# One gather column in 56 moved from GpSimd's indirect DMAs to SyncE, row by row

## The reference

```python
z = h @ W_fc.T                       # 12500 x 64
z_src, z_dst = z[src], z[dst]        # 200000 x 64 each
a = z_src @ blk[0] + z_dst @ blk[K] + ex @ w_e + ...      # moments add a constant
att = jnp.where(a > 0, a, SLOPE * a)
m = jax.ops.segment_max(att, dst, num_segments=N)
expv = jnp.exp(att - m[dst])
w = expv / jax.ops.segment_sum(expv, dst, num_segments=N)[dst]
return jax.ops.segment_sum(w[:, None] * (z_src + ez), dst, num_segments=N)
```

## Time and profile before

| what | value |
|---|---|
| median of 3 runs | 4289.09 us (4285.36 to 4289.59) |
| the profiled execution | 4292.92 us |
| its span, first to last instruction | 4291.0 us |
| mean granted TensorE clock | 0.551 |
| busy in the span: PE, PE loads, DVE, ACT, POOL | 55%, 45%, 71%, 49%, 71% |
| POOL's gathers in the attention pass | 2267.4 to 4233.2 us |

### The profile page before, as it was taken

The page is one execution under the profiler, slowest core; times in us unless marked ns, Lnnn a source line. Parts: engine busy times, 40 slices in busy tenths (PEclk is TensorE's granted clock), DMA queues, the critical chain, the costliest instruction groups (busy, mean ns, idle before and its releaser), DMA issues.

```text
span 4291.0 us, 59828 instructions
## 1 busy us (share of the span) xinstructions
PE 2349.2 (55%) x12446; PEld 1922.5 (45%) x12447; DVE 3028.6 (71%) x9415; ACT 2107.1 (49%) x8940; POOL 3028.7 (71%) x3157
## 2 busy tenths in 40 slices
PE   4566666676878787889986333333333333333332
PEld 1344445554666676768866332222222222222222
DVE  8775556666677777878755777777767777777776
ACT  2778777777776877732042333333333333333332
POOL 5777777777777777777106777777777777777773
PEclk6665565555555565655587555555555555555555
DMA  8653333333444454544302222222222222222222
GB/s 231 166 142 100 91 83 79 91 88 83 95 97 95 96 110 95 114 98 104 67 15 41 37 37 36 36 36 35 36 36 36 36 36 36 35 36 36 36 35 81
DMA packets 726909, 308.31 MB, mean 72 GB/s; under 512 B 661869, under 2 KB 662029, under 8 KB 726480
## 3 DMA queue, kind: packets, MB, share of 16 engines
q1 hardware_dynamic: 612608, 160.26, 18.9%
q0 software_dynamic: 100032, 105.80, 12.0%
q10 hardware_dynamic: 13968, 39.17, 2.7%
HBM read 206.21 MB, written 98.73 MB: 71 GB/s over the span
## 4 chain that ended last, share of the span: by engine, by line
POOL 49%; issue 20%; PE 13%; DVE 9%; ACT 5%; DMA 3%; DVEq 1%; POOLq 0%; SPq 0%; ACTq 0%
POOL zg L637 30%; POOL sorted_dram L599 19%; PE half_banks L958 8%; DVE work L1304 2%; DMA z_sb<-sorted_dram 2%; ACT z_sb L694 1%; PE half_banks L1105 1%; DMA sorted_dram<-ea_sb,idx 1%; DVE oh_all L1228 1%; ACT ohp L710 1%; ACT ohj L712 1%; ACT half_banks L817 1%; PE half_banks L1040 1%; DVEq L1293 1%; DVE zg L1317 1%
## 5 line engine op out<-in xcount | busy, mean ns | idle before, releaser
L599 POOL DMA_INDIRECT sorted_dram<-ea_sb,idx x1563 | 1520.8, 973 | 504.1 <-issue 462.2
L637 POOL DMA_INDIRECT zg<-z_dram,idx x1563 | 1488.1, 952 | 520.7 <-issue 519.4
L958 PE MATMUL half_banks<-z_sb,zg 128*128 128x65 f32 x4736 | 1038.4, 397 | 407.8 <-DVE work L1304 398.1
L958 PEld LDWEIGHTS half_banks<-z_sb,zg 128*128 128x128 f32 x4736 | 987.2, 308 | 580.3 <-DVE zg L1317 568.5
L817 ACT ACTIVATE half_banks<-half_banks,f_s 128x80 f32<-128x80 f32 x1568 | 358.6, 316 | 764.6 <-DVE half_banks L1631 764.6
L1116 PE MATMUL low_banks<-ident,f_top 128*80 128x128 f32 x196 | 85.4, 436 | 1051.6 <-DVE f_top L1664 1051.6
L694 ACT ACTIVATE z_sb<-z_sb 128x98 f32<-128x98 f32 x1568 | 420.4, 270 | 407.0 <-DVE z_sb L1246 407.0
L1304 DVE TENSOR_TENSOR work<-work,half_banks 128x65 f32 x2368 | 510.6, 216 | 151.9 <-PE half_banks L958 67.7
L710 ACT ACTIVATE ohp<-trow,zg 128x128 bf16<-128x128 f32 x1568 | 476.9, 386 | 198.4 <-PE half_banks L936 198.4
L1116 PEld LDWEIGHTS low_banks<-ident,f_top 128*80 128x80 f32 x196 | 27.9, 142 | 1089.6 <-DVE f_top L1664 1089.6
L1317 DVE TENSOR_TENSOR zg<-half_banks,away 128x256 f32<-128x256 f32 x1184 | 492.9, 417 | 1.4 <-issue 0.7
(11 more groups left out here) (288 smaller groups left out, 3407.9 us busy)
## 6 DMA issues: line engine op xcount, KB each, us to landing
z_sb<-sorted_dram SPq DMA_DIRECT2D x592, 132.0 KB
ea_sb<-in_edge_attr_dram SPq DMA_DIRECT2D x195, 256.0 KB, 3.6
sorted_dram<-ea_sb,idx POOLq DMA_INDIRECT x1563
zg<-z_dram,idx POOLq DMA_INDIRECT x1563, 2.5
sorted_dram<-big_b ACTq DMA_DIRECT2D x4, 3333.0 KB, 19.8
sorted_dram<-big_b ACTq DMA_DIRECT2D x4, 3069.0 KB, 11.7
f_t<-t_dram SPq DMA_DIRECT2D x196, 40.0 KB, 2.9
sorted_dram<-big_b ACTq DMA_DIRECT2D x4, 1353.0 KB, 10.7
```

Source lines behind the costliest of these rows:

```text
L599: g_.indirect_dma_start(out=sorted_dram[BUF[c]][:, :], out_offset=bass.IndirectOffsetOnAxis(ap=idx[0:n, m % 4, g:g + 1], axis=0), in_=ea_s ...
L637: g_.indirect_dma_start(out=zg[0:n, s, g, 0:ZW + 1], out_offset=None, in_=z_dram[:, :], in_offset=bass.IndirectOffsetOnAxis(ap=idx[0:n, s, ...
L958: ins = t_.matmul(banks[4 + n % 2][:, u * AW:(u + 1) * AW], oh_step[:, n % 2, u, :], es_sb[:, n % 4, u, 0:AW], start=True, stop=True)
```

## The change

In blocks of seven macros from the third block on (macro 14 and later, 26 blocks of 28), the last column (g = 7) of slot 1 is no longer fetched by POOL. SP fetches its 128 rows one by one, each with a DMA of its own whose address is in a register, into a buffer `row_z` (two halves, used in turn) in `ea_sb`, which is unused by then. ACT copies the 128x66 floats from there into the slot of `zg`, and DVE's `masks` waits for that copy in slot 1. The row numbers come from the input `src` by a small DMA into `row_ids`, one for each block.

The rows of a block are spread over the seven macros before the one that uses them: ROWS_IN[s] rows between the load of the table and the wait for `f_tabn`, ROWS_OUT[s] rows between the store and the wait for its landing.

```diff
+ROWS_IN, ROWS_OUT = (12, 12, 12, 12, 8, 8, 8), (8, 8, 8, 8, 8, 8, 8)
+        row_z = ea_sb[:, 2, 0:2, :]
+        row_ids = ea_sb.rearrange("p s g c -> p (s g c)")[0:1, 3 * G * EW:3 * G * EW + 2 * P].bitcast(I32)
...
+            def load_ids(j):
...
+                    sp.dma_start(row_ids[:, k * P:(k + 1) * P], ids.rearrange("(a p g) -> a p g", a=1, g=G)[:, :, G - 1]
+                                 ).then_inc(r_ids, 16)
+
+            def fetch_rows(k, p0, n):
+
+                for p in range(p0, p0 + n, 4):
+                    rows = nc.values_load_multi_w_load_instructions(
+                        row_ids[0:1, k * P + p:k * P + p + 4], [mybir.EngineType.SP], min_val=0, max_val=NODES - 1)[1]
+                    for u in range(4):
+                        sp.dma_start(row_z[p + u:p + u + 1, k, :], z_dram[bass.ds(rows[u], 1), :]).then_inc(r_land[k], 16)
+
+            def update_rows(it, q, fetch=None):
                 m = it * U + q
                 row = row_of(m)
                 sp.dma_start(tab[0:W, :], tab_dram[bass.ds(row, W), :]).then_inc(f_rows, 16)
+                if fetch is not None:
+                    k, s = fetch
+                    fetch_rows(k, sum(ROWS_IN[:s]) + sum(ROWS_OUT[:s]), ROWS_IN[s])
                 sp.wait_ge(f_tabn, m + 1)
+                sp.sem_inc(s_held[1], 1)
                 sp.dma_start(tab_dram[bass.ds(row, W), :], tab[0:W, :]).then_inc(f_tabs, 16)
+                if fetch is not None:
+                    fetch_rows(k, sum(ROWS_IN[:s + 1]) + sum(ROWS_OUT[:s]), ROWS_OUT[s])
                 sp.wait_ge(f_tabs, m * 16 + 16)
                 sp.sem_inc(s_held[1], 1)
...
+                with sp.Fori(1, NM // U - 1) as it:
                     for q in range(U):
                         load_t(it, q)
-                        update_rows(it, q - 3)
+                        if q == 0:
+                            sp.wait_ge(r_ids, it * 32)
+                            sp.sem_inc(s_held[1], 1)
+                            sp.wait_ge(r_copy, it * 2)
+                            sp.sem_inc(s_held[1], 1)
+                            load_ids((it * 2 + 2, 0))
...
+                        update_rows(it, q - 3, (1 - q // SL, q % SL))
...
-                for g in range(LG + 1 if last else G):
+                n_col = LG + 1 if last else G - 1 if by_rows else G
+                for g in range(n_col):
...
+            def copy_rows(it, q):
+
+                k = q // SL
+                act.wait_ge(r_land[k], it * (16 * P))
+                act.wait_ge(s_zfree, it * U + q + 2)
+                a_.activation(zg[:, 1, G - 1, 0:ZW + 1], row_z[:, k, :], ACT.Copy).then_inc(r_copy, 1)
+
             def act_step(it, q, first=False):
                 add_s(it, q)
                 if not first or q >= 2:
                     factors(it, q - 2)
                 if not first or q >= 1:
                     exps(it, q - 1)
+                if q % SL == 0 and not first:
+                    copy_rows(it, q)
...
                 dve.wait_ge(s_zg[q % SL], (it * 2 + q // SL) * (16 * G) + 16 * G)
+                if q % SL == 1 and not first:
+                    dve.wait_ge(r_copy, it * 2 + 1 + q // SL)
```

More of the change, by code:

```diff
@@ L57 @@
 FAR_ROW = float(1 << 20)
+ROWS_IN, ROWS_OUT = (12, 12, 12, 12, 8, 8, 8), (8, 8, 8, 8, 8, 8, 8)
+assert sum(ROWS_IN) + sum(ROWS_OUT) == P
 FIRST = MS[0] + 1
@@ L290, in gnn_kernel @@
         s_idx = sem("s_idx")
-        s_held = [sem(f"s_held{k}") for k in range(4)]
+        s_held = [sem(f"s_held{k}") for k in range(3)]
         s_pool = sem("s_pool")
@@ L340, in gnn_kernel @@
         s_rows = sem("s_rows")
+        r_ids = sem("r_ids")
+        r_land = [sem(f"r_land{k}") for k in range(2)]
+        r_copy = sem("r_copy")
         s_mask = sem("s_mask")
@@ L369, in gnn_kernel @@
         f_tabs = sem("f_tabs")
-        f_link = [sem(f"f_link{k}") for k in range(5)]
+        f_link = [sem(f"f_link{k}") for k in range(4)]
         s_res = sem("s_res")
@@ L520, in load_t @@
                              ).then_inc(f_trow[q % 2], 16)
-            def update_rows(it, q):
+            def load_ids(j):
+                k = j % 2 if isinstance(j, int) else j[1]
+                m = (j if isinstance(j, int) else j[0]) * SL + 1
+                ids = src[m * ME:m * ME + ME] if isinstance(m, int) else src[bass.ds(m * ME, ME)]
+                with nc.allow_non_contiguous_dma(reason="one id in eight"):
+                    sp.dma_start(row_ids[:, k * P:(k + 1) * P], ids.rearrange("(a p g) -> a p g", a=1, g=G)[:, :, G - 1]
[7 more added lines that the diff above has]
+            def update_rows(it, q, fetch=None):
                 m = it * U + q
@@ L531, in _ @@
             with sp.If(far == 0):
+                load_ids(2)
                 for q in range(U):
                     load_t(0, q)
+                    if q == SL:
+                        sp.wait_ge(r_ids, 16)
+                        load_ids(3)
                     if q >= 3:
-                        update_rows(0, q - 3)
-                with sp.Fori(1, NM // U) as it:
+                        update_rows(0, q - 3, (0, q - SL) if q >= SL else None)
+                with sp.Fori(1, NM // U - 1) as it:
                     for q in range(U):
                         load_t(it, q)
-                        update_rows(it, q - 3)
+                        if q == 0:
[4 more added lines that the diff above has]
+                            load_ids((it * 2 + 2, 0))
+                        if q == SL:
+                            sp.wait_ge(r_ids, it * 32 + 16)
+                            sp.sem_inc(s_held[1], 1)
+                            sp.wait_ge(r_copy, it * 2 + 1)
+                            sp.sem_inc(s_held[1], 1)
+                            load_ids((it * 2 + 3, 1))
+                        update_rows(it, q - 3, (1 - q // SL, q % SL))
+                last = NM // U - 1
+                for q in range(U):
+                    load_t(last, q)
+                    if q == 0:
+                        sp.wait_ge(r_ids, last * 32)
+                        sp.wait_ge(r_copy, last * 2)
+                    update_rows(last, q - 3, (1, q) if q < SL else None)
                 for q in range(3):
@@ L542, in _, with far_macro @@
             with sp.If(far == 1):
-                with sp.Fori(0, NM) as m:
+                def far_macro(m):
                     c0 = sp.snap(sp.value_load(cum_i[0:1, bass.ds(m, 1)], min_val=0, max_val=NM * NB))
@@ L558, in _ @@
                         sp.sem_inc(s_held[1], 1)
+                sp.sem_inc(r_copy, 2)
+                with sp.Fori(0, 2 * SL) as m:
+                    far_macro(m)
+                with sp.Fori(2, NM // SL) as j:
+                    load_ids((j, 0))
+                    sp.wait_ge(r_ids, j * 16 - 16)
+                    sp.sem_inc(s_held[1], 1)
+                    sp.wait_ge(s_zfree, j * SL + 2)
+                    sp.sem_inc(s_held[1], 1)
+                    for p in range(0, P, 4):
+                        rows = nc.values_load_multi_w_load_instructions(
+                            row_ids[0:1, p:p + 4], [mybir.EngineType.SP], min_val=0, max_val=NODES - 1)[1]
+                        for u in range(4):
+                            sp.dma_start(zg[p + u:p + u + 1, 1, G - 1, 0:ZW + 1], z_dram[bass.ds(rows[u], 1), :]
+                                         ).then_inc(r_land[0], 16)
+                    sp.wait_ge(r_land[0], j * (16 * P) - 32 * P + 16 * P)
+                    sp.sem_inc(r_copy, 1)
+                    with sp.Fori(0, SL) as s:
+                        far_macro(j * SL + s)
             for c in range(NB // CZ):
@@ L628, in _, with gather @@
             pool.wait_ge(s_zst, 16 * (NB // CZ))
-            def gather(it, s, last=False):
+            def gather(it, s, by_rows=False, last=False):
                 pool.wait_ge(s_zg_used, it * SL + s + 1)
@@ L639, in gather @@
                         in_offset=bass.IndirectOffsetOnAxis(ap=idx[0:n, s, g:g + 1], axis=0)
-                        ).then_inc(s_zg[s], 16 * (G - LG) if last and g == LG else 16)
-            with pool.Fori(0, NM // SL - 1) as it:
+                        ).then_inc(s_zg[s], 16 * (G - n_col + 1) if g == n_col - 1 else 16)
+            for it in range(2):
                 for s in range(SL):
                     gather(it, s)
+            with pool.Fori(2, NM // SL - 1) as it:
+                for s in range(SL):
+                    gather(it, s, by_rows=s == 1)
             for s in range(SL):
-                gather(NM // SL - 1, s, s == SL - 1)
+                gather(NM // SL - 1, s, by_rows=s == 1, last=s == SL - 1)
         @block.scalar
@@ L1614, in _, with masks @@
             far = dve.snap(dve.value_load(far_i[0:1, 0:1], min_val=0, max_val=1))
-            def masks(it, q):
+            def masks(it, q, first=False):
                 m, col = it * U + q, (it * U + q) * G
@@ L1689, in dve_step @@
             def dve_step(it, q, first=False):
-                masks(it, q)
```

(1 more changed line is left out.)

11 lines of the change are left out of this document (6 added, 5 removed).

## The result

| | median of the runs | ratio to before, 95% interval |
|---|---|---|
| before | 4287.23 us (4282.92 to 4289.59, 4 runs) | |
| after | 5899.12 us (5897.80 to 5901.32, 4 runs) | 1.3762 (1.3745 to 1.3779) |

The kernel became slower by 1612 us. The way was as forecast, the size was not: the forecast was 931 us more. The range ended at 5900 us, and 5899.12 us is only just under that; as a ratio the end is 1.3756 (5900 over 4289.09, the median before at the time), and the measured 1.3762 lies just beyond it.

The account below looks back on a forecast made before the run. POOL's gather issue was taken as the bound; SP would replace it at 104.7 us a block against 68.9, 931 us more over 26 blocks. 4292.9 + 931 - 3.8 gave 5220 us, range 4450 to 5900.

Parts of the forecast that it names:

- POOL is relieved of 32.5 us, on the path: POOL's gathers: 26 blocks each drop one column of 1.25 us, all of it showing if nothing else became the bound.
- ACT's copy and DVE's wait for it cost nothing: One 128x66 copy per block behind ACT's exponent, ending about when DVE asks: counted nothing, at most 8 us without cover.
- SP becomes the bound, by its serial stream: SP's queue: a block needs 104.7 us where POOL needs 68.75, so 931 us more; 75 in 100.
- My rival of a backed-up queue: SP's row DMAs: issues take 0.54 us instead of 0.22, a row 0.97, giving 6285 us; 10 in 100.
- The price of a row, 0.65 us: SP's cost per fetched row: issue 0.22, address and move 0.13, gap 0.04, plus load shared by four and check.
- the middle: SP's row cost taken between one check for four rows, 0.55 us, and each value checked alone, 0.77: 0.65 us.
- My own upper count, 0.77: SP's row cost with each value checked alone at 0.3 us: 0.77 us a row, giving 5619 us.
- a dearer pitch: SP's row cost at the loop's pitch, 0.14 us more on the dearer count: 0.91 us a row, giving 6085 us.
- The fixed part, 21.5 us a block: SP's work besides the rows: 20.3 us for seven macros and 1.2 us for the ids' load, waits and increments.
- The range: Whole kernel time from 4450 us (0.42 us a row) to 5900 us (0.85 us a row).
- dispatch of some 50 ns: Skill's sequencer figure, for the other DMA path: 0.05 for 0.22 us makes a row 0.48 us, the time 4654 us.
- What the profile after would show: SP's waits at L527 and L529 gone, stores about 15 us apart, DVE waiting for f_t and tab, POOL busy half.

Follow-up runs that it names:

- the relief alone: Changed kernel with POOL's 26 columns left out, SP fetching no rows and ACT copying none: 4257.73 us, ratio 0.9932 to before.
- the constant-address kernel: Changed kernel with the same 128 one-row DMAs a block from constant addresses, without register loads, checks or address instructions: 4256.39 us, ratio 0.9929 to before.
- the checks alone: Changed kernel without the bounds checks of the fetched row numbers: 5011.27 us, ratio 1.169 to before.
- three DMAs in four: Changed kernel fetching only the first of each four rows, all register loads and checks kept: 4820.76 us, ratio 1.1246 to before.
- the same 80 rows: Changed kernel without checks, one load a place, 80 rows a block on SP, 48 on ACT: 4405.2 us all ahead, 4257.34 us with four of twelve behind the store.
- the kernel with fewer loads: Changed kernel without checks and with one register load for all 8 or 12 rows of a place: 4822.67 us, ratio 1.1249 to before.

## Why the prediction went wrong

**POOL is relieved of 32.5 us, on the path.** Right. 28.7 us measured with the relief alone, nearly nine tenths of it.

**ACT's copy and DVE's wait for it cost nothing.** Borne out by the constant-address kernel, which has both and loses nothing against the one without the copy (4256.4 and 4257.7 us).

**SP becomes the bound, by its serial stream.** Right, and shown three ways: 128 constant-address DMAs a block cost nothing, the checks alone 888 us, three DMAs in four 1078 us. My rival of a backed-up queue is refuted: the issue took 0.228 us, as the 0.22 taken from L397 in the earlier trace rows said, and 0.295 at most in 3328; the 0.542 and 0.885 us of L869 did not recur.

**The price of a row, 0.65 us: here the prediction failed.** Measured 3.3/4 = 0.83 us. The step was "The 0.15 us FUSED_REGOPS follows straight on the load and is likely in part its latency, so that later checks would be cheaper. I take the middle". All four checks of a group take 0.26 us each, so a row carries 0.26 and not the 0.18 that the middle stood for. The second part is the load: 0.55 us behind a row's DMA where the earlier trace rows have 0.27 and I took 0.3, with its gap a further 0.07 a row. Address, move, issue and gaps came to 0.41 against 0.39. My own upper count, 0.77, was the right reading of the rows, short by the longer load. The 1.24 us of the earlier trace rows, from which I took a dearer pitch still, was the longest of the six such pairs from 3000 to 3060 us; the others take 1.10 to 1.19. By the blocks: 128 x (0.83 - 0.65) = 23 us, over 26 blocks 600 us. The span grew by 1605 us where 931 were forecast, so this step is nearly all of the 674 missing; the next one brings 26 x 4 = 104, and the last macros, which find their slots filled, give some back (near the end seven intervals between stores in a row are 8.8 to 9.1 us, where before most are 10).

**The fixed part, 21.5 us a block.** 131.5 - 128 x 0.83 = 25.3 us. Without rows it was right: POOL's relief alone has 21.9. What is more comes with the rows. Some 1.4 of the 4 us is row_of's load, fourteen times a block, which here has a median of 0.37 us where it had 0.272. Part may be instruction fetch, as the instruction queue moved 3.42 MB instead of 1.85; that was not tested.

```profile
L516 SPq TENSOR_LOAD <-base_i x340: 270/370/460, 2417.7 to 5589.3; - x170
```

**The range.** It ended at 0.85 us a row with a fixed part of 21.5. Both misses have the same sign, and the upper end was a cut through the rival of the queue instead of the dearer count (0.77, or 0.91 with the loop's pitch), whose 6085 us would have covered it. The Trainium skill's dispatch of some 50 ns ("DMA: Bandwidth & Descriptors", "Anatomy of one DMA — SWDGE (gpsimd) path") is stated for the other path, and SP's issue did not follow it: the trace after has 0.228 us.

**What the profile after would show.** The waits at L527 and L529 gone, DVE waiting for the table, POOL's wait for slots: as said. The stores came 18.8 us apart, not 15, the rows 0.83 on average and not 0.65, and POOL was busy 39% of the stretch and not half. DVE's wait at L1631 for f_t, named as well, is not among the long ones; the table's load alone holds it.

## What to carry to other kernels

A sequencer that stands idle 70% of the time is not free: add up its own instructions, one by one, before work is given to it, and count each check and each register load at its full price. Here a 0.23 us DMA cost 0.83 us with what its address needs, and no gain was to be had above 0.37. Work put on a queue goes where that queue stands anyway, behind the store as well as ahead of the wait: the same 80 rows took 148 us less with a third of them behind the store.

## What the runs showed of the hardware

- SP's register load costs by the number of registers and by what precedes it. Behind the table's load four registers take 0.31 us (the trace after), eight 0.53 and twelve 0.76 (the kernel with fewer loads), at the median. Behind the table's store four take 0.50 and eight 0.725; behind a one-row DMA four take 0.55. One register took 0.272 us before; the first of a macro takes 0.45 where rows stand before it. Why it is longer behind rows and the store is open.
- A bounds check is 0.26 us of SP's time for each value, more than the issue of the DMA that it guards (0.228 us).
- SP issued one-partition DMAs of 264 bytes with constant addresses 0.3 us apart, twelve in a row, without a sign of backing up.
- In three sessions whole programs took 25 to 33% longer, the first layer too, where POOL's scatter took 0.962 us a record against 0.963, with longer idle time between. The cause is open.

The loads of four in the changed kernel, by source:

```profile
L538 SPq TENSOR_LOAD <-ea_sb x832: 299/547/741, 2380.8 to 5781.1; - x167
```
